# First attention: turned queries and keys with the head innermost, one product per head's scores

## The reference

```python
q = (hidden_states @ Wq).reshape(B, Sq, H, D)          # 16 sequences, 128 queries, 16 heads, D = 128
k = (encoder_hidden_states @ Wk).reshape(B, Skv, H, D) # 128 keys in each sequence
v = (encoder_hidden_states @ Wv).reshape(B, Skv, H, D)
q, k = rmsnorm(q, gq), rmsnorm(k, gk)
scores = jnp.einsum('bqhd,bkhd->bhqk', q, k) * scale
attn = jax.nn.softmax(scores, axis=-1)
out = jnp.einsum('bhqk,bkhd->bqhd', attn, v)
return out.reshape(B, Sq, H * D) @ Wo
```

## Time and profile before

| what | us |
|---|---|
| median of three runs | 1988.04 |
| the runs | 1986.86, 1989.33, 1988.04 |
| the profiled execution: its span, first to last instruction | 1985.1 |
| of it, first attention (first and last score) | 30.8 to 729.7 |

### The profile page before, as it was taken

The page is one execution under the profiler, slowest core; times in us unless marked ns, Lnnn a source line. Parts: engine busy times, 40 slices in busy tenths (PEclk is TensorE's granted clock), DMA queues, the critical chain, the costliest instruction groups (busy, mean ns, idle before and its releaser), DMA issues. The chain is left out here.

```text
span 1985.1 us, 35876 instructions
## 1 busy us (share of the span) xinstructions
PE 1935.9 (98%) x13552; PEld 1562.9 (79%) x13552; DVE 1315.2 (66%) x2493; ACT 742.2 (37%) x2275; POOL 564.5 (28%) x705
## 2 busy tenths in 40 slices
PE   6999999899999999999999899999999999999999
PEld 4888888778888878888888677777688888888887
DVE  6656655665555654343345599988868878888786
ACT  5555455654555543111122344444433222122211
POOL 3322222322223425310121343433310222322231
PEclk9999999999999999999999899999999999999999
DMA  6632333433444433020122100000112546555654
GB/s 233 221 103 90 99 114 108 165 112 117 137 148 143 144 107 128 27 80 32 32 69 93 63 28 18 21 23 19 54 54 70 191 154 210 192 192 167 201 163 160
DMA packets 126294, 222.39 MB, mean 112 GB/s; under 512 B 17392, under 2 KB 72688, under 8 KB 126192
## 3 DMA queue, kind: packets, MB, share of 16 engines
q1 hardware_dynamic: 102480, 134.01, 20.5%
q0 software_dynamic: 23712, 87.04, 13.2%
HBM read 170.16 MB, written 50.86 MB: 111 GB/s over the span
## 5 line engine op out<-in xcount | busy, mean ns | idle before, releaser
L2385 POOL DMA_INDIRECT m_ring<-in_table,m_row x128 | 127.3, 994 | 370.0 <-DVE l_x_all L2498 264.1
L48 PE MATMUL four_banks<-l_yT_hi,m_hi 128*128 128x512 f32 x512 | 199.4, 389 | 0.0
L48 PE MATMUL four_banks<-l_yT_lo,m_hi 128*128 128x512 f32 x512 | 199.2, 389 | 0.0
L1147 DVE TENSOR_SCALAR f_relu<-bank,f_b 128x512 f32<-128x512 f32 x64 | 48.0, 750 | 166.3 <-ACT f_h_hi L1090 166.3
L529 ACT ACTIVATE prob<-four_banks,mx,rms 128x128 f32<-128x128 f32 x256 | 114.0, 454 | 114.3 <-DVE mx L667 114.3
L328 POOL TENSOR_TENSOR rms<-ssq,constants 128x4 f32<-128x4 f32 x128 | 34.9, 273 | 391.9 <-ACT junk_k L518 237.9
L1090 ACT ACTIVATE f_h_hi<-bank,f_b 128x512 fp32r<-128x512 f32 x64 | 44.2, 690 | 255.6 <-PE bank L48 255.6
L331 POOL TENSOR_TENSOR rms<-rms,constants 128x4 f32<-128x4 f32 x128 | 130.1, 1016 | 10.0
L48 PEld LDWEIGHTS four_banks<-l_yT_hi,m_hi 128*128 128x128 f32 x512 | 96.1, 188 | 20.1 <-issue 0.2
L48 PEld LDWEIGHTS four_banks<-l_yT_lo,m_hi 128*128 128x128 f32 x512 | 96.1, 188 | 20.0
L2362 ACT ACTIVATE m_act_of<-m_dot,l_ln_y 128x2 f32<-128x2 f32 x64 | 19.0, 297 | 238.6 <-DVE m_junk L2488 238.6
(11 more groups left out here) (316 smaller groups left out, 5410.2 us busy)
## 6 DMA issues: line engine op xcount, KB each, us to landing
turned<-blocks SPq DMA_DIRECT2D x64, 512.0 KB, 2.9
qkT<-turned SPq DMA_DIRECT2D x64, 512.0 KB, 4.3
f_stage<-in_w POOLq DMA_DIRECT2D x14, 512.0 KB, 4.6
f_x_in<-x SPq DMA_DIRECT2D x18, 256.0 KB, 3.5
ctx_in<-in_ctxT SPq DMA_DIRECT2D x32, 128.0 KB, 2.6
x_in<-in_x SPq DMA_DIRECT2D x16, 256.0 KB, 2.7
x<-xres SPq DMA_DIRECT2D x16, 256.0 KB, 2.1
x<-l_x_all SPq DMA_DIRECT2D x16, 256.0 KB
```

Of the source, the lines that this page charges most:

```text
L48: mm = pe.matmul(out, st, mv, start=first and n == 0, stop=last and n == len(terms) - 1)
L1147: dve.tensor_scalar(relu[m % 2][:], bank[HB[m % 2]][:], b12[:, layer, m:m + 1], 0.0, ALU.add, ALU.max).then_inc(S["relu_ready"], 1)
L2385: pool.indirect_dma_start(ring[slot][:], None, table, bass.IndirectOffsetOnAxis(ap=row[:, tile_of(g), k:k + 1], axis=0)).then_inc(S[f"got{ ...
```

## The change

The tiles `blocks` and `qkT` get the head as their innermost dimension: `[P, 4, 32, 2 G]` instead of `[P, 4, 2 G, 32]`. The transposes of VectorE write their result with 8 floats (32 bytes) between neighbours. The two transfers move the same bytes in runs of the same length. In `qkT` the 128 tokens of a head lie now 32 bytes apart at one even distance, so that `score` makes one product for each head, with 128 queries as weights and 128 keys as moving columns, both read with that distance: 4 products in place of 16 for a group.

```diff
--- before.py
+++ after.py
@@ -129,8 +129,8 @@
 
 
     k_sb = sb("k_sb", [P, G * D], F32)
-    blocks = [sb(f"blocks{g}", [P, 4, 2 * G, 32], F32) for g in range(2)]
-    qkT = [sb(f"qkT{g}", [P, 4, 2 * G, 32], F32) for g in range(2)]
+    blocks = [sb(f"blocks{g}", [P, 4, 32, 2 * G], F32) for g in range(2)]
+    qkT = [sb(f"qkT{g}", [P, 4, 32, 2 * G], F32) for g in range(2)]
     v_sb = [sb(f"v_sb{g}", [P, G * D], F32) for g in range(2)]
     junk = {n: sb("junk_" + n, [P, slots, D], mybir.dt.bfloat16) for n, slots in (("q", G), ("k", 2 * G))}
     prob = [sb(f"prob{g}", [P, G, P], F32) for g in range(2)]
@@ -256,12 +256,12 @@
         def send(s, g):
             sp.wait_ge(*at(f"k_blocks{g}", s))
             sp.wait_ge(*at(f"q_blocks{g}", s))
-            sp.dma_start(turned[g].rearrange("p (j b) r -> (p j) (b r)", b=4), blocks[g][:].rearrange("p b h i -> p (b h i)")
+            sp.dma_start(turned[g].rearrange("p (j b) r -> (p j) (b r)", b=4), blocks[g][:].rearrange("p b i h -> p (b i h)")
                          ).then_inc(S[f"qk_stored{g}"], 16)
 
         def bring(s, g):
             sp.wait_ge(S[f"qk_stored{g}"], 16 * (s + 1))
-            sp.dma_start(qkT[g][:].rearrange("d p h i -> d p (h i)"), turned[g].rearrange("p d r -> d p r")
+            sp.dma_start(qkT[g][:].rearrange("d p i h -> d p (i h)"), turned[g].rearrange("p d r -> d p r")
                          ).then_inc(S[f"qk_loaded{g}"], 16)
 
         def step(s, second_half=True, storing=True):
@@ -414,10 +414,9 @@
                 pe.wait_ge(*at("q_squared1", s))
             elif there(s - 1):
                 pe.wait_ge(*at("oT_lo1", s - 1))
+            rows = qkT[g][:].rearrange("d p i h -> d (p i) h")
             for j in range(G):
-                for p in range(4):
-                    out = bank[(1, 3)[g]][32 * p:32 * (p + 1), j * P:(j + 1) * P].rearrange("q (p i) -> q p i", p=4)
-                    mm = pe.matmul(out, qkT[g][:, p, j, :], qkT[g][:, :, G + j, :], start=True, stop=True)
+                mm = pe.matmul(bank[(1, 3)[g]][:, j * P:(j + 1) * P], rows[:, :, j], rows[:, :, G + j], start=True, stop=True)
             mm.then_inc(S[f"scored{g}"], 1)
 
         def turn_p(s, g):
@@ -645,9 +644,12 @@
         def blocks_of(heads):
             return heads.rearrange("p (h b i) -> p b h i", h=G, b=4)
 
+        def turned_into(g, heads):
+            return blocks[g][:, :, :, heads].rearrange("p b i h -> p b h i")
+
         def turn_q(s, g):
             dve.wait_ge(*at(f"q_made{g}", s))
-            dve.transpose(blocks[g][:, :, 0:G, :], blocks_of(bank[(7, 3)[g]][:])).then_inc(S[f"q_blocks{g}"], 1)
+            dve.transpose(turned_into(g, slice(0, G)), blocks_of(bank[(7, 3)[g]][:])).then_inc(S[f"q_blocks{g}"], 1)
 
         def norm_and_turn_k(s, g):
             dve.wait_ge(*at(f"k_rms{g}", s))
@@ -657,7 +659,7 @@
                 n = dve.scalar_tensor_tensor(k_sb[:, c], bank[(4, 5)[g]][:, c], rms[g][:, 0, G + j:G + j + 1], gains[:],
                                              ALU.mult, ALU.mult)
             then(n)
-            dve.transpose(blocks[g][:, :, G:2 * G, :], blocks_of(k_sb[:])).then_inc(S[f"k_blocks{g}"], 1)
+            dve.transpose(turned_into(g, slice(G, 2 * G)), blocks_of(k_sb[:])).then_inc(S[f"k_blocks{g}"], 1)
 
         def maxima(s, g):
             dve.wait_ge(*at(f"scored{g}", s))
```

## The result

The changed kernel takes 2102.30 us, the median of four runs (2095.27 to 2104.25), against 1988.68 us for the kernel before, the median of its four. The ratio is 1.0566, with a 95% interval of 1.0546 to 1.0587: slower by 5.7%, some 114 us, where 12 us less were forecast. The profiled execution has a span of 2093.5 us, 108.4 more than the earlier trace rows, in a run of 2095.27 us.

The account below looks back on a forecast made before the run. TensorE's list was taken as the bound, with the first group's transfer landing some 0.2 us from it. A mean gain of 0.40 us over 31 repeats, 12.3 us off 1988.04, gave 1975.7 us; range 1967 to 2016.

Parts of the forecast that it names:

- What bounds the kernel: First attention: TensorE's list of work bounds; the transfer of turned heads lands some 0.2 us from being the bound.
- The strided operands: Score products reading weights and columns 32 bytes apart: price unknown, between nothing and 0.86 us a score; nothing was taken.
- the first end: Strided reads in the scores cost nothing, so a score is priced like the mixing, 1.35 instead of 1.67 us.
- the other end: Each load of a score's weights takes twice its time: 108 ns on each of 8 instructions, 0.86 us a score.
- The transposes: VectorE's four transposes a step, written 32 bytes apart: between 0 and 0.26 us more each; 0 was taken.
- I take 0: The choice that strided writes add nothing to VectorE's four transposes a step, rather than 0.26 us each.
- the angles: VectorE's rows writing 32 values 16 bytes apart; the shortest took 197 ns, read as 1.0 ns a value.
- The sum: Per step, TensorE's loop shortens 0.55 us, the chain to the landing 0.23; mean gain 0.40, over 31 repeats 12.3 us.
- The rivals: Other outcomes: all of TensorE's gain kept (1967.5 us), slow strided reads (0.19), slow strided writes (0.11), no change (0.08).
- reads alone: Rival: strided reads slow TensorE's loads and products in each score by 0.54 us, 34.6 us in all; chance 0.19.
- writes alone, doubled: Rival's harder form: strided transposes take twice 1.04 ns a value, 0.53 us more each, 54 us; slow writes' chance 0.11.

Follow-up runs that it names:

- the experiment on the distance: Scores from other tile places: group 0 weights, group 1 columns read 4, 8, 16, 32 bytes apart; transposes write 8 or 16 apart; 2021.49 us, single run.

## Why the prediction was wrong

- *What bounds the kernel* was right: the first score's landing is some 0.2 us from being the bound. With dense products every regular step ended in it, with slower transposes a step grew by nearly all that they cost (1.53 of 1.63 us), and an earlier return of the first group alone only moved the bound.
- *The strided operands* is one of the two steps that failed: "I take the first end". The price was 126 ns an instruction by the distance of the products (238 ns against 112 with dense operands, medians over the starts in first scores), a little above the other end, 108; a score's bracket became 2.35 us, 1.00 more than the 1.35 of the forecast. The argument that f32 products want a column only every 0.9 ns did not hold: columns 16 bytes apart already put the products 0.21 to 0.23 us apart.
- *The transposes* is the other: "I take 0". The nearest row, the angles at 16 bytes, was read as showing that the stride brings an operation to about 1.0 ns a value, the transposes' own rate. A transpose at 16 bytes is 386 ns longer than at 8, 0.75 ns on each of 512 values, so the price comes on top of the rate. At 32 bytes it was 0.50 us on each transpose from SBUF (1207 against 711 ns), and the four made the chain 1.69 us longer a step. The row of the angles had 32 values and three of its four instances were disturbed, which the text named as its weak point. Why its shortest instance shows so little stays open.
- *The sum* had one term wrong beyond the strides: the first score's gain on the chain is 0.11, not 0.23 us. The run with dense products, the nearest to the change without strides, gained 5 us, not 12.
- *The rivals* had both mechanisms, their places and about their prices: reads alone 2022.6 forecast, 2034.28 measured; writes alone, doubled, 2042 forecast, 2036.14 measured. They were given as alternatives. One distance, 16 bytes, begins the price of both, so they came together, and the upper end of 2016 held neither. Reads and writes alone make some 94 us of the 114 (46.1 and 47.5, by the shown ratios on 1988.68). That sum comes near in part by luck, for together they do not act as alone: alone, the reads cost on TensorE's list, 1.35 us a step; with the writes beside them they cost on the chain, 0.98 and 0.28, while TensorE waits. The lowered clock, 17 us in the profiled execution, was in no rival.

## What to carry to other kernels

Before a layout is turned so that an operand becomes strided, look at the distance in bytes: here, in float32, 8 bytes cost nothing and 16 bytes nearly the full price, for weights, moving columns and VectorE's writes alike. Two rivals that rest on one rule of the hardware are one case with their prices added, and the range has to hold the sum. An operation on the chain to a transfer that is just in time costs nearly all that it grows by, and moving such a transfer forward can delay its neighbour.

## What was not expected of the hardware

Reading weights and columns both 32 bytes apart costs hardly more than one of them: products 238 ns apart with both, 238 with weights alone and 231 with columns alone (medians over their starts, here and in the experiment on the distance), as if the two reads went on side by side. What a send of 512 KB takes beside a return hangs on which is issued first: the second send took 5.1 us when it was issued 0.48 us behind the first return, 4.0 us when 1.15 us behind, and 2.9 us when 0.44 us ahead of it. And in eleven steps of 31 TensorE's granted clock fell to 1.2 GHz after a wait of about 1 us and a strided score. In the regular steps of the other runs it did not fall: not with waits as long (0.99 and 0.95 us) before scores without strides, in the run with strided writes alone, and not with strided scores and no waits, in the run with strided reads alone. What sets the eleven steps apart from the rest of the changed kernel's stays open.
